# Reordering the lead of a fused attention and FFN kernel: chunk 0's projections ahead of chunk 1's turns, chunk 2's turns among the values, statistics tile by tile

## The reference

```python
x = L0_attn_x                                   # (2, 1024, 512) float32
xn = _layernorm(x, axis=-1)
# attention: 32 query heads of 16, 8 groups of keys and values, causal
q = xn @ Wq; kv = xn @ Wkv                      # (512, 512), (512, 256)
weights = softmax(where(causal, -inf, q k^T) / 4)
s = (weights v) @ Wo + bo
# FFN with low-rank parts of rank 16, hidden width 1376
gate = xn @ gate_w.T + (xn @ gate_a.T) @ gate_b.T
up   = xn @ up_w.T   + (xn @ up_a.T) @ up_b.T
hidden = silu(gate) * up
g = silu(hidden @ down_w.T + (hidden @ down_a.T) @ down_b.T)
return x + s * g
```

## Time and profile before

| | us |
|---|---|
| median of 3 runs | 947.27 |
| lowest, highest | 938.77, 950.02 |
| profiled execution | 946.66 |
| its span in the trace | 944.9 |
| PE busy in it | 896.9 (95%) |
| DVE busy | 583.7 (62%) |
| ACT busy | 488.5 (52%) |
| POOL busy | 314.7 (33%) |

### The profile page before, as it was taken

The page is one execution under the profiler, slowest core; times in us unless marked ns, Lnnn a source line. Parts: engine busy times, 40 slices in busy tenths (PEclk is TensorE's granted clock), DMA queues, the critical chain, the costliest instruction groups (busy, mean ns, idle before and its releaser), DMA issues.

```text
span 944.9 us, 21107 instructions
## 1 busy us (share of the span) xinstructions
PE 896.9 (95%) x8075; PEld 633.1 (67%) x8075; DVE 583.7 (62%) x1688; ACT 488.5 (52%) x990; POOL 314.7 (33%) x316
## 2 busy tenths in 40 slices
PE   3898999999999999999999999999889999999997
PEld 3765667676766666667676766554667777777885
DVE  7756666666666666665656565777666666650136
ACT  3522656565555656565656565656445454546211
POOL 4231235252525343525252434441121313121133
PEclk9978999999999999999999999998999999999999
DMA  9466343333333342424242434347565647415774
GB/s 290 165 193 192 92 129 97 122 97 114 108 115 110 97 130 83 137 71 148 58 138 84 126 99 121 100 142 204 155 183 156 171 124 194 137 53 171 205 216 142
DMA packets 142946, 129.20 MB, mean 137 GB/s; under 512 B 36176, under 2 KB 104368, under 8 KB 142624
## 3 DMA queue, kind: packets, MB, share of 16 engines
q1 hardware_dynamic: 142848, 127.87, 45.6%
HBM read 74.07 MB, written 53.22 MB: 135 GB/s over the span
## 4 chain that ended last, share of the span: by engine, by line
PE 88%; DVE 5%; DMA 3%; ACT 2%; issue 2%; SPq 1%; DVEq 0%
PE bank L1011 27%; PE o L1182 14%; PE bank L1045 12%; PE s L1146 10%; PE st L1165 8%; PE bank L286 4%; PE bank L287 4%; PE bank L288 4%; DMA ring<-in_L_attn_x 2%; PE bank L986 1%; PE bank L990 1%; DMA q<-scratch_q 1%; DVE junk L1723 1%; PE s L1153 1%; ACT prob L1442 1%
## 5 line engine op out<-in xcount | busy, mean ns | idle before, releaser
L1442 ACT ACTIVATE prob<-st 128x512 f32<-128x512 f32 (+1 forms) x640 | 323.2, 554 | 263.4 <-PE st L1165 262.8
L1723 DVE CUSTOM_DVE_ANT_0 junk<-s,mask 128x128 bf16<-128x128 f32 (+3 forms) x512 | 229.1, 487 | 69.7 <-PE s L1146 67.9
L1726 DVE TENSOR_REDUCE part_max<-s 128x1 f32<-128x512 f32 x256 | 164.0, 682 | 116.3 <-PE s L1146 116.1
L1146 PE MATMUL s<-k,q 64*128 64x512 f32 (+3 forms) x768 | 150.7, 379 | 12.2 <-DVE part_max L1723 4.6
L567 POOL TENSOR_SCALAR_AFFINE_SELECT prob<-prob 128x512 f32<-128x512 f32 x128 | 81.8, 652 | 225.8 <-ACT prob L1442 224.3
L1011 PE MATMUL bank<-x_hi,w_hi 64*128 64x512 f32 (+1 forms) x704 | 150.2, 412 | 2.4 <-DVE hid L1564 1.1
L1182 PE MATMUL o<-prob,v 128*32 128x512 f32 (+3 forms) x1536 | 145.4, 497 | 0.0
L1011 PE MATMUL bank<-x_lo,w_hi 64*128 64x512 f32 (+1 forms) x704 | 142.8, 391 | 0.0
L1011 PE MATMUL bank<-x_hi,w_lo 64*128 64x512 f32 (+1 forms) x704 | 142.1, 389 | 0.0
L1165 PE MATMUL st<-q,k 64*128 64x512 f32 (+3 forms) x768 | 130.7, 356 | 2.3 <-ACT prob L1442 1.8
L1146 PEld LDWEIGHTS s<-k,q 64*128 64x128 f32 x768 | 79.1, 188 | 53.6 <-DVE part_max L1723 24.4
(11 more groups left out here) (148 smaller groups left out, 1089.0 us busy)
## 6 DMA issues: line engine op xcount, KB each, us to landing
late_context_hid_in<-scratch_hid SPq DMA_DIRECT2D x16, 1408.0 KB, 7.2
q<-scratch_q SPq DMA_DIRECT2D x60, 200.0 KB
scratch_hid<-tanh_hid_hi SPq DMA_DIRECT2D x40, 256.0 KB, 2.1
scratch_hid<-hid_lo SPq DMA_DIRECT2D x40, 256.0 KB, 2.4
scratch_o<-o_sb SPq DMA_DIRECT2D x32, 256.0 KB
scratch_q<-proj_hi SPq DMA_DIRECT2D x30, 256.0 KB
k<-scratch_k SPq DMA_DIRECT2D x30, 192.0 KB
x_again<-in_L_attn_x SPq DMA_DIRECT2D x16, 256.0 KB, 4.4
```

Source lines behind the costliest of these rows:

```text
L1146: pe.matmul(sb_[(p + odd) % S_BANKS][:, 0:wd], q[half, g % 2, h // 2, qt * P:(qt + 1) * P], k[half, g % 2, k0:k0 + wd], start=True, stop=T ...
L1442: nc.scalar.activation(prob[:, job % 3, h, 0:JOB_COLS[j]], st[at % ST_BANKS][:, 0:JOB_COLS[j]], ACT.Exp, scale=float(HD) ** -0.5).then_inc ...
L1723: ins = dve.tensor_tensor_reduce(junk[:, n % S_BANKS, 0:wd], bank_[:, 0:wd], mask[:, C - wd:C], 1.0, LOWEST, ALU.add, ALU.max, part[:, h, ...
L1726: ins = dve.tensor_reduce(part[:, h, qt, dst:dst + 1], bank_[:, 0:wd], AX.X, ALU.max)
```

## The change

The background order changes on all engines. Chunk 0's keys and first query block are projected ahead of chunk 1's turns; two of chunk 2's turns stand behind value 0 and value 1, then comes (0,1), then chunk 2's other two turns, (2, keys) and value 2; chunk 3 stays as it was. The first twelve bank entries have a table of their own (FIRST_BANKS), and a turn's bank of chunk 1 is freed by its low part, which now waits for ACT's copy as well. On ACT the copy of chunk 1's turns stands beside their rounding, and the query weights are rounded in other places. On DVE chunk 1 is normalised behind the low parts of chunk 0; the statistics of chunk 3 are four single tiles, behind value 0, turn (2,0), value 1 and (0,1), the last of them with the aggregates; chunk 3 is normalised behind the low part of (2, keys); `low_of_low_b` goes from chunk 2's turns to chunk 3's, and `low_of_low_a` two steps into (0,2). On SP `load_first` stands behind `load_x(3)`. The scores of the first group begin in slot 6 as those of the others.

```diff
-FIRST_OF_ALL = 10
@@ bank_order
     for c in range(2):
         for k in range(KT):
             yield "turn", c, k
-    for c, blk in LEADING:
-        yield "proj", c, blk
-    for c in range(2):
-        yield "value", c, 0
-    for c in BESIDE:
-        for k in range(KT):
-            yield "turn", c, k
-        yield ("proj", *BESIDE[c])
-        yield "proj", c, KEYS_BLOCK
-        yield "value", c, 0
+        for blk in (KEYS_BLOCK, 0):
+            yield "proj", c, blk
+
+    yield "value", 0, 0
+    yield "turn", 2, 0
+    yield "value", 1, 0
+    yield "turn", 2, 1
+    yield ("proj", *BESIDE[2])
+    for k in range(2, KT):
+        yield "turn", 2, k
+    yield "proj", 2, KEYS_BLOCK
+    yield "value", 2, 0
+    for k in range(KT):
+        yield "turn", 3, k
+    yield ("proj", *BESIDE[3])
+    yield "proj", 3, KEYS_BLOCK
+    yield "value", 3, 0
@@ bank_places
+FIRST_BANKS = [0, 1, 2, 3, 4, 5, 6, 7, 0, 1, 5, 6]
-        elif u < 8:
-            used = (u,)
+        elif u < len(FIRST_BANKS):
+            used = (FIRST_BANKS[u],)
@@ read_out
-            return dict(turn=(xT_copied if a else xT_lo, KT * a + b + 1),
+            return dict(turn=(xT_copied if a >= 2 else xT_lo, KT * a + b + 1),
@@ stream_slots
-            first = FIRST_UNIT if g else FIRST_OF_ALL
-            even = SLOTS * g + first + (UNIT_SLOTS + FIRST_UNIT - first) * sum(weight[:w]) // sum(weight)
+            even = SLOTS * g + FIRST_UNIT + UNIT_SLOTS * sum(weight[:w]) // sum(weight)
@@ SP background
                     load_x(2 + c)
-                for c, blk in LEADING:
-                    yield STEPS["proj"]
-                    store_projection(c, blk)
-                    if (c, blk) == (0, 0):
+                    if c == 1:
                         load_first()
+                    for blk in (KEYS_BLOCK, 0):
+                        yield STEPS["proj"]
+                        store_projection(c, blk)
@@ PE score_pair, scores_t
-                    pe.wait_ge(xT_copied, 2 * KT)
                     pe.wait_ge(xT_lo, KT)
+                    pe.wait_ge(p_lo, 1)
+                elif at == 0:
+                    pe.wait_ge(p_lo, 4)
@@ ACT copy_x
-                elif c:
-                    act.wait_ge(xT_lo, KT * c + kt + 1)
@@ ACT background
+                round_query_weights(0)
+                for blk in (KEYS_BLOCK, 0):
+                    yield STEPS["proj"]
+                    split_projection(0, blk)
                 for kt in range(KT):
                     yield STEPS["turn"]
                     round_x(1, kt)
+                    copy_x(1, kt)
+                yield STEPS["proj"]
+                split_projection(1, KEYS_BLOCK)
+                root(2)
+                split_low_b()
+                yield STEPS["proj"]
+                split_projection(1, 0)
+                round_query_weights(1)
@@ DVE low_x
-                if c == 0:
-                    dve.wait_ge(xT_copied, kt + 1)
+                dve.wait_ge(xT_copied, KT * c + kt + 1)
@@ DVE background
+                statistics(0)
+                normalise_x(0)
+                statistics(1)
                 for c in range(2):
                     for kt in range(KT):
                         yield STEPS["turn"]
                         low_x(c, kt)
+                    if c:
+                        statistics(2)
+                    else:
+                        normalise_x(1)
+                    for blk in (KEYS_BLOCK, 0):
+                        yield STEPS["proj"]
+                        low_projection(c, blk)
+                        if c and blk == KEYS_BLOCK:
+                            normalise_x(2)
+                for c in range(2):
+                    yield STEPS["value"]
+                    tile_statistics(3, 2 * c)
+                    yield STEPS["turn"]
+                    if c == 0:
+                        tile_statistics(3, 1)
+                yield STEPS["proj"]
+                low_projection(*BESIDE[2])
+                variance(3, tile_statistics(3, TT - 1))
+                yield (KT - 2) * STEPS["turn"]
+                yield STEPS["proj"]
+                low_projection(2, KEYS_BLOCK)
+                normalise_x(3)
+                yield STEPS["value"]
+                for kt in range(KT):
+                    yield STEPS["turn"]
+                    low_of_low_b(kt)
...
                 for c, blk in AFTER[:SOON]:
-                    yield STEPS["proj"]
+                    yield 2
+                    low_of_low_a()
+                    yield STEPS["proj"] - 2
                     low_projection(c, blk)
```

More of the change, by code:

```diff
@@ L505, in read_out @@
                 return (gate_read, NCH * a + b + 1), (up_read, NCH * a + b + 1)
-            return dict(turn=(xT_copied if a else xT_lo, KT * a + b + 1), proj=(p_lo, (kind == "proj" and projection(a, b)) + 1), value=(v_copied, a + 1),
+            return dict(turn=(xT_copied if a >= 2 else xT_lo, KT * a + b + 1), proj=(p_lo, (kind == "proj" and projection(a, b)) + 1), value=(v_copied, a + 1),
                         fold=(w_lo, 2 * a + b + 1), down_fold=(d_lo, a + 1), down=(y_done, a + 1),
@@ L779, in background @@
                     store_value(c)
[L780 to L789 removed]
+                    yield STEPS["turn"]
+                yield STEPS["proj"]
+                store_projection(*BESIDE[2])
+                yield (KT - 2) * STEPS["turn"]
+                for n in range(4):
+                    load_raw(n)
+                yield STEPS["proj"]
+                store_projection(2, KEYS_BLOCK)
+                yield STEPS["value"]
+                store_value(2)
+                yield KT * STEPS["turn"]
+                for n in range(4, 8):
+                    load_raw(n)
+                yield STEPS["proj"]
+                store_projection(*BESIDE[3])
+                yield STEPS["proj"]
+                store_projection(3, KEYS_BLOCK)
+                yield STEPS["value"]
+                store_value(3)
                 for c, blk in AFTER[:SOON]:
@@ L1092, in background @@
                         yield from turn_x(c, kt)
-                for c, blk in LEADING:
-                    yield from project(c, blk)
+                    for blk in (KEYS_BLOCK, 0):
+                        yield from project(c, blk)
                 for c in range(2):
                     yield from value(c)
-                for c in BESIDE:
-                    for kt in range(KT):
-                        yield from turn_x(c, kt)
-                    yield from project(*BESIDE[c])
-                    yield from project(c, KEYS_BLOCK)
-                    yield from value(c)
+                    yield from turn_x(2, c)
+                yield from project(*BESIDE[2])
+                for kt in range(2, KT):
+                    yield from turn_x(2, kt)
+                yield from project(2, KEYS_BLOCK)
+                yield from value(2)
+                for kt in range(KT):
+                    yield from turn_x(3, kt)
+                yield from project(*BESIDE[3])
+                yield from project(3, KEYS_BLOCK)
+                yield from value(3)
                 for c, blk in AFTER[:SOON]:
@@ L1356, in background @@
                     copy_value(c)
-                for c in BESIDE:
-                    for kt in range(KT):
-                        yield STEPS["turn"]
-                        round_x(c, kt)
-                        copy_x(c, kt)
-                    yield STEPS["proj"]
-                    split_projection(*BESIDE[c])
-                    yield STEPS["proj"]
-                    split_projection(c, KEYS_BLOCK)
-                    yield STEPS["value"]
-                    copy_value(c)
+                    yield STEPS["turn"]
@@ new lines, in background @@
+                    round_x(2, c)
+                    copy_x(2, c)
+                yield STEPS["proj"]
+                split_projection(*BESIDE[2])
+                for kt in range(2, KT):
+                    yield STEPS["turn"]
+                    round_x(2, kt)
+                    copy_x(2, kt)
+                root(3)
+                yield STEPS["proj"]
+                split_projection(2, KEYS_BLOCK)
+                for blk in range(2, NBLK - 1):
+                    round_query_weights(blk)
@@ L1368, in background @@
+                yield STEPS["value"]
+                copy_value(2)
+                for kt in range(KT):
+                    yield STEPS["turn"]
+                    round_x(3, kt)
+                    copy_x(3, kt)
+                yield STEPS["proj"]
+                split_projection(*BESIDE[3])
+                yield STEPS["proj"]
+                split_projection(3, KEYS_BLOCK)
+                yield STEPS["value"]
+                copy_value(3)
                 split_low_a()
@@ L1622, in background @@
             def background():
-                for c in range(2):
-                    statistics(c)
-                    normalise_x(c)
+                statistics(0)
```

(2 more changed lines are left out.)

74 lines of the change are left out of this document (24 added, 50 removed).

## The result

| | before | changed |
|---|---|---|
| median us | 945.46 (4 runs, 938.77 to 950.02) | 954.97 (4 runs, 952.01 to 957.79) |
| profiled execution | 946.66 | 957.79 |
| span in the trace | 944.9 | 956.1 |

The ratio is 1.0108, with a 95% interval of 1.0065 to 1.0150: the changed kernel is 1.1% slower, 10.2 us on the median of before (the medians themselves differ by 9.5). The forecast was +2 us, 948.7, with a range of 941 to 955, and the median lies at its upper end. The sign was right, the size was not.

What follows compares the result with a forecast made beforehand. TensorE's in-order queue was taken as the bound, through its idle time and clock. The end of (0,2), 40.15 + 45.03 + 8.65 + 3.4 = 97.2 against 94.94, less 0.3, gave +2.0: 948.7 us, range 941 to 955.

Steps and rivals of the forecast that it cites:

- part 1: Chunk 0's keys before chunk 1's turns: 3.0 us idle before project(1, keys), clock falls (65%), projections end 4.55 us later.
- part 2: First scores in slot 6 instead of 10: loads there at 41.2, scores at 46.2, cost 0.
- first keys late: Rival at the first scores: chunk 3's megabyte ahead of load_first makes them wait until 51; 953 us, 8%.
- part 3: Chunk 2 between: new waits of 2.1 and 2.55 us around (0,1), about 0.9 at slot 22, 0.1 among values.
- part 4: Chunk 3, low_of_low_b beside its turns: waits of 0.6 at turns, 1.5 at slot 28, 0.9 behind (1,1).
- part 5: low_of_low_a two steps later: the 2.36 us idle and the clock fall behind it gone; cost 0, or 1.2.
- the first step of the prediction: Only the stretch from 12.43 to 94.94 us, ending with (0,2), changes; all behind it moves rigidly.
- The clock behind the lead: Around the end of (0,1), 4.65 us idle in some 6 bring one 6.83 us stretch at 1.2 GHz, 3.4 lost.
- a longer slow time: Rival in chunk 3: part 4's waits take the clock once more, 3.4 to 5.1 us; 953 us, 16%.

Runs made afterwards that it cites:

- variance_later: Changed kernel with the last tile's statistics and aggregates of chunk 3 behind chunk 2's last two turns: ratio to before 1.0081.
- turns_ahead: Changed kernel with the last two turns of chunk 2 ahead of query projection (0,1) instead of behind it: ratio to before 1.0050.
- lead_alone: Kernel before with only chunk 0's keys and queries ahead of chunk 1's turns, first scores still in slot 10: ratio to before 1.0050.
- copies_behind: Changed kernel with ScalarE's four copies of chunk 1 behind its roundings, VectorE's low parts waiting for the rounding alone: ratio to before 1.0064.
- lead_undone: Changed kernel with the lead of the kernel before, all behind it as changed: ratio to before 1.0149.
- repaired: Changed kernel with (0,0) behind chunk 1's turns, chunk 2's last turns ahead of (0,1), low_of_low_b among value 3's steps: ratio to before 1.0007.
- keys_early: repaired with chunk 3's turns ahead of value 2, (3, keys) ahead of (1,1), chunk 3's normalisation and last statistics in single tiles: ratio to before 0.9985.
- low_b_later: Changed kernel with the four pieces of low_of_low_b among the steps of value 3 instead of beside chunk 3's turns: ratio to before 1.0048.
- low_a_alone: Kernel before with only low_of_low_a two steps later on VectorE: ratio to before 1.0006.
- low_b_alone: Kernel before with only low_of_low_b moved, to the steps of value 3: ratio to before 0.9984.

## Why the forecast was right in kind and too small

**The lead (part 1).** The key projection started 6.1 us behind the first turn, as forecast (18.4 - 12.43 = 6.0). The wait ahead of project(1, keys) was forecast at 3.0 us and measured at 3.65: I had taken 0.6 us for each of chunk 1's turns, the length of one, where their starts are 0.44 apart, so PE stood there earlier. The clock fell behind the wait, from 31.16 to 37.99, 3.0 us lost on 6.04 of work against 2.6. The projections ended at 40.26, for 40.15, and that this agrees so well is luck: the first turn was 0.7 us late, and the first key projection took 4.0 us instead of 5.2. I had PE at 1.2 GHz until 23.9, but in this profile the first six matmuls from 19.18 on have the full pace of 0.23, and the clock was low only from 20.9 to 24.2; in variance_later and turns_ahead the same twelve matmuls took 5.3 us, at the low pace throughout. That the clock's fall is not given by the length of the wait is shown by lead_alone (3.65 us, no fall; the other five profiles with that wait have one) and copies_behind (2.06 us, a fall).

**First scores in slot 6 (part 2).** No wait, as forecast. But lead_undone, repaired and keys_early show that it is near its limit: with `load_first` 1.7 to 4.4 us later, counted from the first turn, and PE 2.0 to 5.6 us earlier at the scores, 1.7 to 2.7 us of wait stand there. The rival "first keys late" had part of that: from the issue of the queries' last store to `load_first` it took 5.85 us before and 6.05 in lead_undone, but 7.5 in the changed kernel and 8.5 in repaired and keys_early, where chunk 3's x is issued behind or just ahead of these stores. In the changed kernel it cost nothing.

**Around (0,1) (part 3).** Forecast 2.1 and 2.55 us, measured 3.23 and 2.52. The term that was too small is the one on VectorE, and the trace says why. DVE of the changed kernel behind (0,1):

```profile
56.39 0.68 DVE L1523 BATCH_NORM_STATS2 stats<-ring 128x6 f32<-128x512 f32 x1
57.11 0.38 DVE L1533 BATCH_NORM_AGGREGATE mean_var<-stats 128x2 f32<-128x6 f32 x4
57.52 1.04 DVE L1535 TENSOR_SCALAR small<-mean_var 128x4 f32<-128x4 f32 x1
58.60 0.56 DVE L1774 CUSTOM_DVE_ANT_0 junk<-s,mask 128x384 bf16<-128x384 f32 x1
```

and POOL at the same time:

```profile
57.27 1.26 POOL L602 TENSOR_TENSOR x_lo<-xT,x_hi 128x512 fp32r<-128x512 f32 x1 [4.29 <-ACT xT L1245]
...
71.15 1.28 POOL L607 TENSOR_TENSOR wq_lo<-wq,wq_hi 128x512 fp32r<-128x512 f32 x1 [7.54 <-ACT wq_hi L1250]
```

The operation on four elements takes 0.17 us elsewhere and 1.04 here: it ends at 58.56, with GpSimd's low part at 58.53. That is 0.9 of the 1.1 us that were missing. The same happened in normalise_x(3), a multiplication from 71.40 to 72.45 while GpSimd ran to 72.43, and it makes up the difference between 1.62 us and the forecast 0.9 at slot 22. In both cases GpSimd had begun first. The Trainium skill (SBUF — State Buffer, Who interferes with whom) says that a VectorE instruction with two SBUF inputs contends with a GpSimd instruction that reads SBUF, that a tensor_scalar can do so too when it runs in a 2-port mode, and that there whoever issues first has the ports for the whole instruction and the other is blocked. The multiplication has two SBUF inputs; the operation at 57.52 is a tensor_scalar with one, and in which mode it ran no trace shows. Both ended within 0.03 us of GpSimd's instruction, which agrees. I had counted on such blocking for the four pieces of low_of_low_b and not for the small operations, for which it is much dearer than their own time.

**Chunk 3 (part 4).** Forecast 1.5 us at slot 28, with 0.2 to 4.4 as bounds; measured 2.37, with pieces of 1.32 us on average. low_b_later shows the cause: with the pieces elsewhere that wait is gone. GpSimd paid as well, with 6.39 us for its four low parts of chunk 3 against 5.01 in low_b_later. At slot 31 I had 0.9 us and there was none; PE was at 1.2 GHz there, and in low_b_later, at full clock, 0.79 us stand at that place.

**low_of_low_a (part 5) and the step that failed.** The wait near 86 went, as forecast. What failed is the first step of the prediction, that all behind (0,2) moves rigidly: of the 9.1 us that the forecast was short in the profile, 3.8 arose there, more than in any other term. I looked for who waits for low_of_low_a and for what is late next among the folds, but not at what had been hidden under the idle time: the chain of stores, landing and loads for the second group, which had its slack from this wait and from the low clock. It took back 2.09 us and, by the fall behind it, 1.7 more (3.41 us at half). low_a_alone shows the same on the kernel before, where no gain from the edit is seen.

**The clock behind the lead.** Forecast one stretch of 6.83 us; it was one of 10.23 with 6.87 us of work (3.4 lost, as booked) and a second, 3.40 us, behind the wait of 2.37 in chunk 3 (1.7 lost). That was the rival "a longer slow time", at its lower price.

**The sum again.** +2.0 was forecast for a profile that gained 11.1. The lead ended 0.1 later than forecast. Idle time from there to the end of (0,2) was 2.6 more (11.2 for 8.65): 1.1 around (0,1), 0.9 at slot 22, 0.9 at slot 28, 0.4 among the values, less 0.9 at slot 31. The second time at half clock is 1.7 more, and 0.4 of PE's work there I cannot assign. Behind the end of (0,2) come 3.8, the 2.1 and 1.7 at the second group; the 0.3 to be given back there was given back. Behind the marker come 0.6, where this execution was at half clock for 3.4 us near 855; most profiles of this series show such a stretch at the same code, while before, lead_alone and variance_later do not. 2.0 + 0.1 + 2.6 + 1.7 + 0.4 + 3.8 + 0.6 = 11.2. By the ratio the change cost 10.2.

That the loss lies in these waits and the low clock behind them, taken together, is shown by repaired: with the waits of 3.65, 3.23, 2.52 and 2.37 us shortened or gone and the rest of the change kept, the kernel is back at the time of before. What each is worth alone is shown less well, by the overlap of the intervals.

## What to carry to other kernels

A stall on the bottleneck engine is also slack for everything that runs beside it. Before booking its end as a gain, follow every chain that starts before the stall and is waited for behind it, DMA round trips first: here a landing of 6.1 us took back 2.09 us of a wait of 2.36, and a fall of the clock came with it; repaired (2.52 us ahead of the first scores) and low_b_alone (1.22) show the like. And an order that shortens one wait should be checked for what covered the next one: a turn placed directly ahead of the projection that needs its low part exposes the whole ScalarE, GpSimd chain (2.5 us), where one projection between them hides it.

## What the runs showed of the hardware

- Two small VectorE operations on SBUF took six times as long beside a GpSimd subtraction: 0.17 us became 1.04 and 0.16 became 1.05, each ending with it. The masked maxima, which read their scores from PSUM, kept their 0.69 us. DVE of variance_later, while GpSimd makes a low part from 57.81 to 59.09:

```profile
58.13 0.69 DVE L1774 CUSTOM_DVE_ANT_0 junk<-s,mask 128x512 bf16<-128x512 f32 x1 [0.17 <-PE s L1168]
58.75 0.08 DVE L1774 DVE_READ_ACCUMULATOR2_ANT part_max<- 128x1 f32 x1
58.75 0.69 DVE L1774 CUSTOM_DVE_ANT_0 junk<-s,mask 128x512 bf16<-128x512 f32 x1
```

- The same idle time of 3.65 us before the same matmul was followed by 1.2 GHz in the changed kernel and by full clock in lead_alone, and one of 2.06 us (copies_behind) by 1.2 GHz. So a single profile can't price such a wait to better than the 3 us that the fall cost here; it takes several runs.
- From the issue of the last store of (3, keys) to the load that waited for it took 6.1 us in both traces, 5.3 in repaired and 6.5 in low_a_alone. For the first queries it was 5.85 us before and 8.5 in repaired, with a megabyte of x issued just ahead of the stores.
